# Centring and gate products of three layers laid in four 64x64 corners of the TensorE array

## The reference

```
x = x + layer_l(_gn(x))                      # group norm over the whole image, l = 0..3

# layers 0 to 2 (layer 3 has no input norm, no bias)
xn    = layernorm(x) * w + b                 # over the 64 channels of a pixel
left  = (xn @ Wl + bl) * sigmoid(xn @ Wlg + blg) * mask     # layer 2 has no mask
right = (xn @ Wr + br) * sigmoid(xn @ Wrg + brg) * mask
t     = einsum('bikd,bjkd->bijd', left, right)   # one 192x192x192 product per channel
gate  = sigmoid(xn @ Wog + bog)
out   = layernorm(t) * gate @ Wout
```

## Time and profile before

| | |
|---|---|
| median of three runs | 1425.36 us |
| the profiled execution: its own time | 1427.8 us |
| its span, first to last instruction | 1425.6 us |
| PE busy | 1231.4 us (86%) |
| DVE busy | 983.5 us (69%) |
| ACT busy | 920.8 us (65%) |
| POOL busy | 525.5 us (37%) |
| granted TensorE clock, mean | 0.972 |

### The profile page before, as it was taken

The page is one execution under the profiler, slowest core; times in us unless marked ns, Lnnn a source line. Parts: engine busy times, 40 slices in busy tenths (PEclk is TensorE's granted clock), DMA queues, the critical chain, the costliest instruction groups (busy, mean ns, idle before and its releaser), DMA issues. The chain is left out here.

```text
span 1425.6 us, 39778 instructions
## 1 busy us (share of the span) xinstructions
PE 1231.4 (86%) x11486; PEld 686.5 (48%) x11486; DVE 983.5 (69%) x2692; ACT 920.8 (65%) x1849; POOL 525.5 (37%) x490
## 2 busy tenths in 40 slices
PE   0799998789799998999982999999888788899897
PEld 0455555434344544674331555567544344467443
DVE  6577776368779999226991888842299899931587
ACT  0577775399677777227992888842499677722676
POOL 0355553045355655003551666620155200000365
PEclk9999999999889999999995999999999999999999
DMA  8011111578623332797758555549799544469898
GB/s 296 23 51 50 50 50 64 140 230 263 202 90 105 105 110 84 211 297 217 204 158 326 156 170 176 185 142 298 251 288 282 183 156 155 149 186 313 263 315 267
DMA packets 222432, 258.73 MB, mean 181 GB/s; under 512 B 54177, under 2 KB 209057, under 8 KB 222369
## 3 DMA queue, kind: packets, MB, share of 16 engines
q1 hardware_dynamic: 193920, 232.75, 52.1%
q10 hardware_dynamic: 28448, 25.17, 5.4%
HBM read 139.89 MB, written 117.96 MB: 181 GB/s over the span
## 5 line engine op out<-in xcount | busy, mean ns | idle before, releaser
L1036 DVE SCALAR_TENSOR_TENSOR lr<-ps,mask,act_out 128x128 f32 (+5 forms) x1152 | 278.8, 310 | 51.1 <-ACT act_out L785 42.9
L1195 POOL TENSOR_TENSOR rstd<-ve,half_col 128x6 f32<-128x6 f32 x144 | 190.4, 1323 | 232.0 <-DVE ve L1003 196.5
L1240 POOL TENSOR_TENSOR new_ring<-val,lr 128x384 f32<-128x384 f32 x96 | 104.0, 1084 | 372.1 <-issue 297.8
L569 PE MATMUL ps<-w_parts,val 64*128 64x256 bf16 (+1 forms) x1728 | 199.7, 310 | 18.4 <-DVE lr L1036 17.7
L785 ACT ACTIVATE act_out<-ps 128x384 f32<-128x384 f32 x384 | 176.1, 483 | 50.5 <-PE ps L579 34.3
L1228 POOL TENSOR_TENSOR val<-act_out,gate_ring 128x384 f32<-128x384 f32 x96 | 99.8, 1040 | 224.8 <-ACT act_out L855 189.5
L679 PE MATMUL ps<-in_ring,k 128*128 128x384 f32 x288 | 124.4, 517 | 26.2 <-DMA in_ring<-t_scratch 23.0
L838 ACT ACTIVATE sq<-ps 128x384 f32<-128x384 f32 x192 | 105.7, 551 | 54.0 <-PE ps L679 52.0
L1087 DVE COPY cen<-ps 128x384 f32<-128x384 f32 x48 | 26.8, 558 | 159.1 <-PE ps L637 159.1
L637 PE MATMUL ps<-lr 64*128 64x192 f32 (+3 forms) x896 | 125.8, 331 | 9.8 <-DVE lr L1036 5.2
L761 ACT ACTIVATE cen<-ps,gn 128x384 f32<-128x384 f32 x144 | 83.8, 582 | 77.1 <-PE ps L524 73.8
(11 more groups left out here) (108 smaller groups left out, 2290.0 us busy)
## 6 DMA issues: line engine op xcount, KB each, us to landing
gate_scratch<-gate_ring SPq DMA_DIRECT2D x192, 192.0 KB, 2.2
gate_ring<-gate_scratch SPq DMA_DIRECT2D x96, 384.0 KB, 3.9
lr<-x_scratch SPq DMA_DIRECT2D x72, 384.0 KB, 4.9
in_ring<-t_scratch SPq DMA_DIRECT2D x72, 384.0 KB, 3.9
x_scratch<-new_ring SPq DMA_DIRECT2D x48, 384.0 KB, 3.4
in_ring<-x_scratch SPq DMA_DIRECT2D x96, 192.0 KB, 2.4
lr<-x SPq DMA_DIRECT2D x6, 1536.0 KB, 15.5
t_scratch<-cen SPq DMA_DIRECT2D x96, 96.0 KB, 4.0
```

Of the source, the lines that this page charges most:

```text
L569: mm = nc.tensor.matmul(banks[h][:, :, 0:P], moving(x, s)[half(h), N * r:N * r + P], proj_weights(w, h)[:, 0:2 * P], start=start, stop=sto ...
L1036: ins = nc.vector.scalar_tensor_tensor(out5[:, h, lo // 2:hi // 2, :, m], ps[:, 4 + 2 * r + h, lo:hi].rearrange("p (a e) -> p a e", e=2), ...
L1195: nc.gpsimd.tensor_tensor(rstd[:, s % 2, :], ve[:, s % 2, :], half_col[:, :], ALU.pow)\
```

## The change

The centring product and the gate product of layers 0 to 2 are each laid as four products on the 64x64 corners of the array, 192 columns each. The corner (q, e) takes partitions of half q and columns of picture row e, and writes partition half e of bank q. So after centring, the partitions are picture rows and the columns are halves; the gate product, laid the same way, turns this back. The projections are the same code, so that their subtile r is now a half and their operand half h a picture row, and `glu` writes to the places exchanged accordingly.

Banks 0 and 1 are now both used by every tile: columns 0 to 191 for centring, 192 to 383 for the gate. So `centre(n+4)` waits for the copy `cen(n+3)` and the gate sigmoid of tile n, and `gate(n+1)` waits for the copy `cen(n+4)`. The variance takes bank 3. On PE `centre(n+4)` moves ahead of `project(n,1)`; on ACT `cen(n+4)` moves between the two sigmoids, and the square is made from `cen` in SBUF. PE's tile loop of layers 0 to 2 is written out in full.

```diff
+                def corners(first, weights, x, start, stop):
+
+                    for q in range(2):
+                        for e in range(2):
+                            mm = nc.tensor.matmul(ps[C * e:C * e + C, q, first:first + N], weights[half(q), half(q)],
+                                                  x[half(q), N * e:N * e + N], start=start, stop=stop,
+                                                  skip_group_check=True)
+                    return mm
...
-                    slot_free(pe, a_sq, base + n - 1)
-                    slot_free(pe, a_ve, base + n - 1)
-                    nc.tensor.matmul(ps[:, s % 2, 0:TILE], w_centre[:, :], in_ring[:, s, :] if l else x_all[:, n, :],
-                                     start=True, stop=True).then_inc(a_z, 1)
+                    slot_free(pe, a_cen, base + n)
+                    if gated:
+
+                        pe.wait_ge(a_gate, base + n - RING + 1)
+                    corners(0, w_centre, in_ring[:, s, :] if l else x_all[:, n, :], True, True).then_inc(a_z, 1)
...
+                    if ln:
+                        if centred:
+
+                            pe.wait_ge(a_cen, base + n + RING)
+                        for w, x in passes:
+                            mm = corners(N, gate_weights(w), moving(x, s), (w, x) == passes[0], (w, x) == passes[-1])
+                        mm.then_inc(a_gate_mm, 1)
+                        return
...
                     project(n, s, 0)
+                    if ln and ahead >= 4:
+                        centre(n + 4, i + 1, s, True)
                     project(n, s, 1)
-                    if ln and ahead >= 4:
-                        centre(n + 4, i + 1, s)
...
-                over_tiles(pe, step)
+                if ln:
+
+                    for n in range(TILES):
+                        step(n, n // RING, n % RING, TILES - 1 - n)
+                else:
+                    over_tiles(pe, step)
...
+                def squared(n, s):
+                    act.wait_ge(a_cen, base + n + 1)
                     slot_free(act, a_var, base + n - 1)
-                    nc.scalar.activation(cen[:, s, :], ps[:, s % 2, 0:TILE], ACT.Identity, bias=gn_cb)\
-                        .then_inc(a_cen, 1)
-                    nc.scalar.activation(sq[:, s % 2, :], ps[:, s % 2, 0:TILE], ACT.Square, bias=gn_cb)\
-                        .then_inc(a_sq, 1)
+                    nc.scalar.activation(sq[:, s % 2, :], cen[:, s, :], ACT.Square).then_inc(a_sq, 1)
...
                     sigmoids(n, s, 0)
+                    if ln and ahead >= 4:
+                        centred(n + 4, s)
                     sigmoids(n, s, 1)
                     if ln and ahead >= 4:
-                        centred(n + 4, s)
+                        squared(n + 4, s)
...
                         nc.vector.tensor_tensor(
-                            out5[:, :, :, :, m],
-                            ps[:, 4 + 2 * r:6 + 2 * r, 0:COLS].rearrange("p h (a e) -> p h a e", e=2),
-                            sig.rearrange("p h (a e) -> p h a e", e=2), ALU.mult).then_inc(a_free, 1)
+                            out5[:, r, :, :, bass.ds(ROWS * n, ROWS)].rearrange("p a e g -> p g a e"),
+                            ps[:, 4 + 2 * r:6 + 2 * r, 0:COLS].rearrange("p g (a e) -> p g a e", e=2),
+                            sig.rearrange("p g (a e) -> p g a e", e=2), ALU.mult).then_inc(a_free, 1)
```

More of the change, by code:

```diff
@@ L531, in variance @@
                         for part in (sq_high, sq_low):
-                            mm = nc.tensor.matmul(ps[:, s % 2, TILE + 2 * j:TILE + 2 * j + 2],
+                            mm = nc.tensor.matmul(ps[:, 3, 2 * j:2 * j + 2],
                                                   part[:, s % 2, P * j:P * j + P], sel_bf[:, :],
@@ L542, in spread, with gate @@
                     mm.then_inc(a_bc, 1)
-                def gate(n, s):
+                def gate(n, s, centred):
                     if IN_PARTS[l]:
@@ L593, in step @@
                 def step(n, i, s, ahead):
-                    gate(n, s)
+                    gate(n, s, ahead >= 3)
                     if ln and ahead >= 1:
@@ L604, in phase_a @@
                 if ln:
-                    centre(0, 0, 0)
-                    centre(1, 0, 1)
+                    centre(0, 0, 0, False)
+                    centre(1, 0, 1, False)
                     variance(0, 0)
                     variance(1, 1)
-                    centre(2, 0, 2)
-                    centre(3, 0, 3)
+                    centre(2, 0, 2, False)
+                    centre(3, 0, 3, False)
                     spread(0, 0)
                     variance(2, 2)
-                over_tiles(pe, step)
+                if ln:
[3 more added lines that the diff above has]
+                    over_tiles(pe, step)
             def keep_clock(bank, count):
@@ L759, in centred @@
                     slot_free(act, a_xn, base + n - RING + 1)
+                    nc.scalar.activation(cen[:, s, :].rearrange("p (h j) -> p h j", h=2), ps[:, 0:2, 0:N], ACT.Identity,
+                                         bias=gn_cb).then_inc(a_cen, 1)
+                def squared(n, s):
+                    act.wait_ge(a_cen, base + n + 1)
                     slot_free(act, a_var, base + n - 1)
-                    nc.scalar.activation(cen[:, s, :], ps[:, s % 2, 0:TILE], ACT.Identity, bias=gn_cb)\
-                        .then_inc(a_cen, 1)
-                    nc.scalar.activation(sq[:, s % 2, :], ps[:, s % 2, 0:TILE], ACT.Square, bias=gn_cb)\
-                        .then_inc(a_sq, 1)
+                    nc.scalar.activation(sq[:, s % 2, :], cen[:, s, :], ACT.Square).then_inc(a_sq, 1)
                 def plain(n, i, s):
@@ L776, in gate @@
                     slot_free(act, gate_stored[s], 16 * (l * TURNS + i))
-                    nc.scalar.activation(gate_ring[:, s, :], ps[:, 3, 0:TILE], ACT.Sigmoid, bias=gate_bias[:, 0:1])\
-                        .then_inc(a_gate, 1)
+                    slot = gate_ring[:, s, :].rearrange("p (r j) -> p r j", r=ROWS)
+                    nc.scalar.activation(slot if ln else gate_ring[:, s, :], ps[:, 0:2, N:2 * N] if ln else ps[:, 3, 0:TILE],
+                                         ACT.Sigmoid, bias=gate_bias[:, 0:1]).then_inc(a_gate, 1)
                 def sigmoids(n, s, r):
@@ L807, in phase_a @@
                 if ln:
-                    centred(0, 0)
-                    centred(1, 1)
-                    centred(2, 2)
-                    centred(3, 3)
+                    for n in range(RING):
+                        centred(n, n)
+                        squared(n, n)
                     high(0, 0)
@@ L1002, in var_eps @@
                     slot_free(dve, a_rstd, base + n - 1)
-                    nc.vector.tensor_scalar(ve[:, s % 2, :], ps[:, s % 2, TILE:TILE + 2 * CHUNKS], LN_EPS, None,
+                    nc.vector.tensor_scalar(ve[:, s % 2, :], ps[:, 3, 0:2 * CHUNKS], LN_EPS, None,
                                             ALU.add).then_inc(a_ve, 1)
@@ L1032, in glu @@
                     if HAS_MASK[l]:
-                        for h in range(2):
+                        for g in range(2):
+                            h, row = (r, ROWS * n + g) if ln else (g, m)
                             for t, (lo, hi) in enumerate(((0, P), (P, COLS))):
                                 ins = nc.vector.scalar_tensor_tensor(
-                                    out5[:, h, lo // 2:hi // 2, :, m],
-                                    ps[:, 4 + 2 * r + h, lo:hi].rearrange("p (a e) -> p a e", e=2),
-                                    mask4[:, t, h, bass.ds(m, 1)],
-                                    sig[:, h, lo:hi].rearrange("p (a e) -> p a e", e=2), ALU.mult, ALU.mult)
+                                    out5[:, h, lo // 2:hi // 2, :, row],
+                                    ps[:, 4 + 2 * r + g, lo:hi].rearrange("p (a e) -> p a e", e=2),
+                                    mask4[:, t, h, bass.ds(row, 1)],
+                                    sig[:, g, lo:hi].rearrange("p (a e) -> p a e", e=2), ALU.mult, ALU.mult)
                         ins.then_inc(a_free, 1)
```

3 lines of the change are left out of this document (2 added, 1 removed).

## The result

The changed kernel takes **1443.3 us** (median of 4 runs, 1442.95 to 1444.73); the kernel before took 1424.1 us beside it.

What follows compares the result with a forecast made beforehand. It took PE to bound layer 0, DVE's ring layer 1, PE with the DMA queue close behind layer 2. Terms +2, 0, -4 and -1 us gave -3 from 1425.4, so 1422 us; range for 8 in 10, 1407 to 1436.

Steps and rivals of the forecast that it cites:

- The price of the corners: On PE: centring falls from 0.75 to 0.33 us, layer 0's gate product from 0.73 to 0.49 us.
- the corners share less: Rival, 15%: centring's corners run two at a time, 0.66 us instead of 0.33; 1445 us in all.
- PE was all that mattered: Rival, 3%: layer 0 falls to PE's own work of 3.29 us a tile; 1383 us in all.
- Layer 0: A ring through the delayed second sigmoid and `glu` takes 3.99 us a tile against 3.95; +2 us, bounds -10 and +7.
- DVE can start subtile 1 at 2.31 + 0.53: Layer 0's ring: second sigmoid 2.31 us after the wide part, DVE 0.53 us later, at 2.84 us.
- Layer 1: DVE's closed ring stays at 3.68 us a tile, the second sigmoid 0.2 us early; 0 us, bounds -2 and +5.
- Layer 2: Quicker compute gains only until the DMA queue limits at 3.35 us a tile; -4 us, bounds -1 and -13.
- delivers a pair in 6.70 us whatever the engines do: Layer 2: the DMA queue's ring of keeps and gathers waits for no compute engine, 6.70 us per pair of tiles.
- PE's written-out loop removes its turns: PE's loop, layers 0 to 2: turns vanish; in layer 0 they are in the 3.95 us; no separate term.
- the clock falls: Rival, 5%: PE, less busy in layers 0 and 1, gets half clock for half of layer 1's tiles; +41 us, 1466 us.
- The compute pace of layer 2: Layer 2 were the queue no limit: about 3.1 us a tile from ACT and DVE work plus idling.
- Layer starts: Prologues of the layers: centring 0.4 us shorter, the square waits 0.58 us for `cen` instead of 0.48; together -1 us.

Runs made afterwards that it cites:

- e4: The changed kernel with DVE's tile loop of layer 0 written out as well; 1436.7 us, ratio 1.0072 to the kernel before.
- e1: The kernel before with only PE's tile loop of layers 0 to 2 written out; 1433.5 us, ratio 1.0050 to the kernel before.
- e14: The kernel before with only PE's tile loop of layer 2 written out; 1434.1 us, ratio 1.0052 to the kernel before.
- e13: The kernel before with only PE's tile loop of layer 1 written out; 1425.5 us, ratio 0.9986 to the kernel before.

## Why the prediction was wrong

**The price of the corners: right.** 0.32 us for eight, 0.33 forecast; the gate product of layer 0 holds PE 0.48 us to the transposes, 0.49 forecast. The rival "the corners share less" is out. So is "PE was all that mattered": PE's 3.29 us a tile was reached in no run; over four tiles in mid-layer 3.63 was the least.

**Layer 0: right mechanism, one arc mis-sized.** Forecast 3.99 us, +2 us; measured 4.11 us, +7.5 us. "DVE can start subtile 1 at 2.31 + 0.53" took the 0.53 from written-out tiles; in the runtime loop it is 0.67 us (e4). The earlier trace rows would have given it: DVE starts at 133.99 there, 0.65 us after its sigmoid:

```profile
133.34 0.47 ACT L785 ACTIVATE act_out<-ps 128x384 f32<-128x384 f32 x1
```

That +7.5 us come so near to the bound of +7 is chance: the bound was for centring products behind two waits, and they cost no more than forecast.

**Layer 1: right.** 3.676 us against 3.689, 3.68 forecast.

**Layer 2: the step that failed.** I wrote that the queue "delivers a pair in 6.70 us whatever the engines do", and of the loop "PE's written-out loop removes its turns", at no price. The first step treats the ring of keeps and gathers as closed; the second adds some 20 fetches to the very DMA engines that close it. The ring went to 7.47 us a pair, 3.73 us a tile, and passed the tiles' own pace. Forecast -4 us, measured +8.9 us. The kernel before with this loop written out, in which there are no corners and the gate waits for no `cen`, loses 9.3 us (e1) and 7.9 us (e14) in layer 2 by the traces, with the same ring of 7.47 us in e14. So the term put at nothing is as large as the whole loss; the quicker products, 13.00 us for four tiles instead of 13.57 as long as the gathers are in time, bought nothing behind it. Two more things are in the changed kernel's traces that e14 has less of or not at all: the gate's new wait, for which PE stands 11.1 us in the row of waits above, and 20.5 us at half clock, where e14 has 6.8. What they cost isn't settled: against 7.9 and 9.3 us by the loop alone, the 8.9 us leave nothing that can be told for them and the quicker products together. The rival "the clock falls" named an effect that occurred, but in the wrong layers: layers 0 and 1 idle more and stayed at 1.00 in mid-layer.

**The compute pace of layer 2** was as forecast: the first tiles, before the gathers are late, take 3.25 us each, between my 3.1 and the 3.39 of before.

**Layer starts: not shown.** Forecast -1 us. The first sigmoid came 1.3 us sooner, but it spreads by 3 us over the kernels.

**Between layers 1 and 2** some 3 us more went by than before. Other kernels of the series spread there by as much, and no run was made for it.

## What to carry to other kernels

Unrolling is an edit like another: count the 16 KB blocks that it adds per stretch, and ask which DMA ring with little reserve runs beside them. When a ring of engines holds a layer, look for the next ring before pricing what lies behind the first: here three of 3.62 to 4.11 us stood one behind the other, and each edit only uncovered the next. And take an arc of a ring from tiles that run in the same kind of loop as those that it is to predict.

## What the hardware showed that I had not expected

- A 16 KB instruction block occupied one DMA engine for about 1.35 us in the interval looked at (0.9 to 1.75 us over the layer), and with about one block per pair of tiles the keep-gather ring grew from 6.81 to 7.47 us (e13, e14), about half a block's time for each pair.
- The same stream cost nothing where PE waited for no load: layers 0 and 1 written out take 3.953 and 3.658 us a tile (e1) against 3.945 and 3.689, and layer 1 alone leaves the time at 0.9986 of before (e13).
- In DVE's runtime loop `glu` starts 0.15 us later after the start of the sigmoid that it waits for than in the written-out one (0.67 and 0.52 us).
- Four 64x64 f32 products of 192 columns in different corners run at once: they start within 0.02 us of each other, and eight take 0.32 us.
